# A macaron of attention and sparse layers: the attention body's buffers apart, its norm and q's first part on ScalarE, a PSUM bank cleared sooner, and the first sparse stage's sends in pieces

## Chip, cores and metric

The program runs on one NeuronCore of a Trainium2 chip. The metric is the device time of one execution in microseconds. The core's engines are TensorE (PE), VectorE (DVE), ScalarE (ACT) and GpSimd (POOL), and SyncE (SP), which here only issues DMAs. Each engine runs its own list of instructions in order and waits on semaphores.

## The reference, cut to what matters

Eight sequences of 512 tokens, 128 features, float32. Six stages run one after the other, each on `x + stage(layernorm(x))`: a sparse layer (eight experts of hidden size 512, top 2 of a softmax router), an attention (16 heads of size 8), the sparse layer again, a second sparse layer (16 small experts and a shared one), a state-space layer, and the second sparse layer again. The change touches the first two.

```python
q = (x @ Wq + bq)                      # 16 heads of 8
k = ((x @ Wk + bk) @ Wl + bl)
v = ((x @ Wv + bv) @ Wl + bl)
attn = softmax(q @ k^T * scale); out = (attn @ v) @ Wo + bo
# sparse layer
probs = softmax(xf @ w_router); topk_w, topk_idx = top_k(probs, 2)
h = gelu(xf @ w1[i] + b1[i]); out = sum over the two experts of weight * (h @ w2[i] + b2[i])
```

## The kernel before, in words

`PHASES` lists the stages; each is a function that gives every engine its part of the program. `after_phases` makes an engine wait for the end of the stage before.

**First sparse stage (`moe0_phase`, `occ == 0`).** Tokens are sorted to experts. For each of the eight sequences b, DVE takes the norm's sums (`seq_stats`, step `st`b), POOL makes from them the scale and shift (`seq_root`, four instructions), ACT writes the normalised rows (`seq_xn`, `xn`b), PE transposes them (`seq_T`), ACT copies that out (`seq_copy`, `c`b), PE multiplies by the router weights (`seq_R`) and ACT copies the logits (`seq_logits`, `l`b). The sequences form three groups: 0 and 1; 2 to 4; 5 to 7. For a group DVE picks the top two (`pick_a`, `pick_b`, step `pk`), PE adds up positions (`group_pos`), ACT copies them (`group_copy`, `p`), and DVE computes each token's row in the sorted buffer (`place_a`, `place_b`, step `sl`, L478 to L506) and updates the tables (`place_c`). POOL then sends the group's rows (`group_send`, L535): one indirect DMA for each tile of 128 tokens and each of its two experts, 16, 24 and 24 of them. The buffer was first filled with zeros by a DMA from SP (L2260), for which `group_send` waits (`pads`). The lists PE_STEPS, ACT_STEPS and DVE_STEPS give the order, from which the waits' numbers are made. When all rows have landed, SP loads blocks of 512 rows (`x_load`), 23 in all, and the experts' matmuls run (`up0`, `down0`). Before that DVE splits the expert weights in two parts (`w_lo_dve`, L620).

**Attention (`attn_phase`).** It has two parts. In the first, here called the front, the loop over b runs `pe_a`, `act_a`, `dve_a`, `pool_a` and `sp_a`: POOL gathers the expert results (`gather`, L260), DVE adds them to x (`combine`, L273) and takes the norm's sums (`norm_a`), POOL the root (`norm_b`, L183 and L185), DVE writes the normalised rows (`norm_c`, L215), PE transposes them (`norm_pe`, L223) and multiplies by the weights (L1358, L1364, L1367), ACT adds biases (L1382), and q and k are each split into three bfloat16 parts (`split_q` on DVE, L1401 to L1405; k with its first two parts on ACT, L1411 and L1415, and the rest in `split_k1` and `split_k2`, L1419 and L1423). SP writes the parts to a scratch in DRAM (`saved`) and reads them back rearranged (`load`); for a body it issues 24 such loads, in the first four bodies. Where DVE has time, it already takes row maxima of sequence 0 (`early`, L1596). The second part, the body (`pe_b`, `act_b`, `dve_b`), alternates score matmuls (L1638, L1590), exponentials on ACT (L1646), row maxima on DVE (L1596) and the product with v (`av_pe`, L1656). The tiles of the body (`probs`, `o_sb` and others) lie over the front's (`q_sb`, `parts` and others): `new_part()` frees the latter. So ACT, DVE and POOL wait between the two until the last parts are saved:

```python
for c_ in "qk":
    nc.scalar.wait_ge(saved[c_], 16 * B)
```

PE waits there for `zeroed`, since DVE clears PSUM bank 6 (L1456) behind its last work in the front.

## Time and profile before

| | us |
|---|---|
| median of three runs | 1734.02 |
| the three runs | 1730.81, 1735.60, 1734.02 |
| the profiled execution, its own time | 1741.21 |
| its span | 1739.5 |

The times of rows count from the start of the span. Stages by the trace: routing and sends of the first sparse stage up to 132 us, its experts up to 290, attention's front from 311 to 441, its body from 441 to 852, then the other stages. In a timeline row the brackets hold how long the engine stood idle before the instruction and what released it. Lines are those of the kernel before; the helper's line L535 is the send in both sparse stages.

### The profile page before, as it was taken

Reading aid. Unit: us, or ns where it says so; the run is one execution under the profiler, and the core shown is the slowest. Engines: PE = TensorE matmul, PEld = TensorE weight load, DVE = VectorE, ACT = ScalarE, POOL = GpSimd, SP = SyncE. Lnnn points to the kernel's source line nnn. Section 1 sums busy time; section 2 is a strip of 40 time slices with the busy share of each in tenths; the row PEclk is TensorE's granted clock in tenths of the full one; section 3 lists DMA queues with packets and bytes.
Section 4 is the critical chain, followed back from the end, with each engine's and each line's share of the span. In section 5 each row is a group of like instructions: output and inputs, shape, how many; then the busy total and the mean of one; then the engine's idle time right before and its main releaser. Section 6 shows DMA issues by size and latency. Waiting matters only on the chain. (4 is left out here: it accounts for less than half of the span.)

```text
span 1739.5 us, 20323 instructions
## 1 busy us (share of the span) xinstructions
PE 1292.5 (74%) x6213; PEld 740.0 (43%) x6213; DVE 1227.1 (71%) x2698; ACT 852.9 (49%) x1293; POOL 479.2 (28%) x597
## 2 busy tenths in 40 slices
PE   3208996556788888887539991788798994579998
PEld 3206885222122222222238881555464432446665
DVE  3526995688799999895459984576766665657765
ACT  3206774222677777777437771323333474223332
POOL 3773333761000012222353334434201101111010
PEclk9999998767799999999669995899998855789999
DMA  6152221341111111101222211444340000033444
GB/s 237 59 154 74 81 79 61 96 133 58 38 38 33 35 41 46 38 25 38 68 91 67 86 61 49 91 93 107 78 99 1 0 1 0 1 72 77 98 95 102
DMA packets 83569, 117.31 MB, mean 67 GB/s; under 512 B 16660, under 2 KB 38644, under 8 KB 83468
## 3 DMA queue, kind: packets, MB, share of 16 engines
q1 hardware_dynamic: 75276, 99.28, 21.4%
q0 software_dynamic: 8192, 16.79, 3.4%
q8 instruction: 49, 0.80, 0.2%
q14 instruction: 52, 0.43, 0.1%
HBM read 80.13 MB, written 35.39 MB: 66 GB/s over the span
## 5 line engine op out<-in xcount | busy, mean ns | idle before, releaser
L1596 DVE TENSOR_REDUCE shared<-pair 128x2 f32<-128x1024 f32 x256 | 305.2, 1218 | 28.9 <-PE pair L1590 23.8
L1646 ACT ACTIVATE shared<-pair 128x1024 f32<-128x1024 f32 x256 | 258.8, 1023 | 83.1 <-PE pair L1638 79.5
L730 DVE TENSOR_TENSOR shared<-shared 128x512 fp32r<-128x512 f32 x184 | 175.7, 956 | 30.6 <-ACT shared L720 27.4
L1138 ACT ACTIVATE shared<-pair 128x512 f32<-128x512 f32 x144 | 85.7, 595 | 210.2 <-PE pair L1090 206.2
L535 POOL DMA_INDIRECT xs_rows<-shared,slots x128 | 132.8, 1037 | 128.5 <-ACT shared L1646 78.5
L1149 DVE TENSOR_TENSOR shared<-shared,pair 128x512 f32<-128x512 f32 x128 | 87.5, 684 | 106.2 <-ACT shared L1138 101.1
L1088 PE MATMUL pair<-shared 128*128 128x512 f32 x288 | 149.7, 520 | 17.0 <-DVE shared L1149 16.8
L684 PE MATMUL pair<-shared 128*128 128x512 f32 x368 | 152.9, 415 | 0.0
L1656 PE MATMUL bank<-shared 128*9 128x512 f32 x1024 | 143.1, 632 | 8.8 <-ACT shared L1646 8.7
L714 ACT ACTIVATE shared<-pair,shared 128x512 f32<-128x512 f32 x184 | 126.8, 691 | 43.8 <-PE pair L686 37.5
L260 POOL DMA_INDIRECT staged<-ys_rows,slots x128 | 130.5, 1019 | 61.8 <-issue 36.7
L686 PE MATMUL pair<-shared 128*128 128x512 f32 x368 | 145.7, 396 | 0.0
L685 PE MATMUL pair<-shared 128*128 128x512 f32 x368 | 145.3, 395 | 0.0
L1166 PE MATMUL pair<-shared,down_w 128*128 128x512 f32 x256 | 135.9, 614 | 7.7 <-DVE shared L1156 7.6
L1590 PE MATMUL pair<-shared 48*128 48x512 bf16 x512 | 103.4, 404 | 43.1 <-DVE shared L1596 22.7
L1638 PE MATMUL pair<-shared 51*128 51x512 bf16 x512 | 103.8, 405 | 39.2 <-DVE shared L1596 30.2
L1090 PE MATMUL pair<-shared 128*128 128x512 f32 x288 | 116.9, 406 | 0.0
L1089 PE MATMUL pair<-shared 128*128 128x512 f32 x288 | 116.5, 404 | 0.0
L1638 PEld LDWEIGHTS pair<-shared 51*128 51x128 bf16 x512 | 25.0, 94 | 183.5 <-issue 88.7
L1156 DVE TENSOR_TENSOR shared<-shared 128x512 f32<-128x512 f32 x128 | 87.6, 685 | 10.4 <-DMA shared<-p_coef_rows 10.4
L223 PE MATMUL bank<-ident,xn 128*128 128x128 f32 x128 | 24.5, 324 | 89.8 <-DVE xn L215 87.5
L636 PE MATMUL bank<-ident,shared 128*128 128x128 f32 x184 | 29.5, 286 | 75.5 <-DMA shared<-xs_rows 69.6
(290 smaller groups left out, 2398.1 us busy)
## 6 DMA issues: line engine op xcount, KB each, us to landing
shared<-p_coef_rows SPq DMA_DIRECT2D x64, 512.0 KB, 10.2
shared<-xs_rows SPq DMA_DIRECT2D x46, 256.0 KB, 2.8
ys_rows<-shared SPq DMA_DIRECT2D x46, 256.0 KB, 2.0
xs_rows<-shared SPq DMA_DIRECT2D x1, 5888.0 KB, 20.9
staged<-in_L_ffn_w SPq DMA_DIRECT2D x16, 256.0 KB
shared<-in_L_ffn_w SPq DMA_DIRECT2D x16, 256.0 KB
p_q_parts<-shared SPq DMA_DIRECT2D x8, 384.0 KB
p_k_parts<-shared SPq DMA_DIRECT2D x8, 384.0 KB
```

Source lines behind the costliest of these rows:

```text
L260: g.indirect_dma_start(out=buf[:, at:at + E], out_offset=None, in_=ys_rows, in_offset=bass.IndirectOffsetOnAxis(ap=slots[:, b * TILES + i, ...
L535: g.indirect_dma_start(out=xs_rows, out_offset=bass.IndirectOffsetOnAxis(ap=slots[:, t, k:k + 1], axis=0), in_=xn_rows[occ][:, t, :], in_o ...
L684: nc.tensor.matmul(out_bank, w_hi, x_hi, start=start, stop=False)
L685: nc.tensor.matmul(out_bank, w_hi, x_lo, start=False, stop=False)
L686: return nc.tensor.matmul(out_bank, w_lo, x_hi, start=False, stop=stop)
L730: nc.vector.tensor_tensor(hl[u % RING][:], hid[u % RING][:], hh[u % RING][:], ALU.subtract).then_inc(s["dve_done"], 1)
L1088: nc.tensor.matmul(out_bank, w_hi, x_hi, start=start, stop=False)
L1166: nc.tensor.matmul(bank[4 + b % 2][:], w, hid[t % 4][:], start=(j == 0), stop=(j == IT - 1)).then_inc(s["down_done"], 1)
L1596: nc.vector.tensor_reduce(mneg[:, i, 2 * c:2 * c + 2], pair_of("max", b, m)[:], AX_X, ALU.max, negate=True).then_inc(s["mx_read"], 1)
L1638: last = nc.tensor.matmul(pair_of("exp", b, 2 * st + p)[:, f, :], ka[par][rows, c, kt * P:(kt + 1) * P], qa[par][rows, c, :], start=True, ...
L1646: nc.scalar.activation(probs[st % 2][:, 2 * p:2 * p + 2, :], pair_of("exp", b, 2 * st + p)[:], ACT.Exp, scale=scale).then_inc(s["exp_done" ...
L1656: last = nc.tensor.matmul(bank[6][32 * hh:32 * hh + HD + 1, :], v_all[:, b * TILES + kt, hh % 2 * (H // 2) + g * HG // 2 + hh // 2, :], pr ...
```

## The change

In the first sparse stage DVE takes the sums of all eight sequences first, POOL all eight roots before any send, ACT and PE handle the sequences 0 and 1, then 2 and 3, in pairs, and the sends wait at some places for steps of ACT (`pace`) and, before the third group, for `onehot`. SP waits for the first block's landing before it issues the load of the second, in both expert stages of this kind. In attention the body's tiles no longer lie over the front's, and the waits between the parts go; q's first part (the cast at L1401) moves to ACT (`q1_act`), `norm_c` gives way to `xn_a` on ACT behind `k1_act`, for which POOL makes the shift as well (`shift_a`, two instructions more); the clearing of bank 6 moves ahead of DVE's second group of early maxima; and `load` waits for `saved` in the body.

```diff
@@ -333,11 +333,11 @@
 
 
         GROUPS = (((0, 2), (2, 5), (5, 8)), ((0, 2), (2, 4), (4, 6), (6, 7), (7, 8)))
-        PE_STEPS = ("T0 T1 R0 T2 R1 T3 R2 pos0 T4 R3 T5 R4 T6 R5 pos1 T7 R6 R7 pos2 bias".split(),
+        PE_STEPS = ("T0 T1 R0 R1 T2 T3 R2 pos0 T4 R3 T5 R4 T6 R5 pos1 T7 R6 R7 pos2 bias".split(),
                     "T0 R0 T1 R1 pos0 T2 R2 T3 R3 pos1 T4 R4 T5 R5 pos2 T6 R6 pos3 T7 R7 pos4 bias".split())
-        ACT_STEPS = ("xn0 xn1 c0 xn2 c1 l0 xn3 c2 l1 xn4 c3 l2 p0 xn5 c4 l3 xn6 c5 l4 c6 l5 p1 xn7 c7 l6 l7 p2 th bias".split(),
+        ACT_STEPS = ("xn0 xn1 c0 c1 l0 l1 xn2 xn3 c2 c3 l2 p0 xn4 c4 l3 xn5 c5 l4 xn6 c6 l5 p1 xn7 c7 l6 l7 p2 th bias".split(),
...
@@ -755,18 +755,22 @@
                 if occ == 0:
                     t.wait_ge(pool_chain, 9)
                     t.wait_ge(x_first, 32)
-                    for b in range(B):
-                        if b > 1:
-                            t.wait_ge(s["act_step"], act_at(occ, f"c{b - 2}"))
+                    seq_T(occ, 0, bank[0])
+                    seq_T(occ, 1, bank[1])
+                    seq_R(occ, 0, bank[2])
+                    seq_R(occ, 1, bank[3])
+                    t.wait_ge(s["act_step"], act_at(occ, "c0"))
+                    seq_T(occ, 2, bank[0])
+                    for b in range(3, B):
+                        t.wait_ge(s["act_step"], act_at(occ, f"c{b - 2}"))
                         seq_T(occ, b, bank[b % 2])
-                        if b:
-                            if b > 2:
-                                t.wait_ge(s["act_step"], act_at(occ, f"l{b - 3}"))
-                            seq_R(occ, b - 1, bank[2 + (b - 1) % 2])
+                        t.wait_ge(s["act_step"], act_at(occ, f"l{b - 3}"))
+                        seq_R(occ, b - 1, bank[2 + (b - 1) % 2])
                         if b == 3:
                             group_pos(occ, 0, bank[4])
                         if b == 6:
                             group_pos(occ, 1, bank[5])
+                    t.wait_ge(s["act_step"], act_at(occ, f"l{B - 3}"))
                     seq_R(occ, B - 1, bank[3])
                     group_pos(occ, 2, bank[4])
@@ -798,18 +802,19 @@
             def scalar(c_):
                 after_phases(c_, n)
                 if occ == 0:
-                    for b in range(B):
-                        if b != B - 1:
-                            seq_xn(occ, b)
-                        if b in (0, B - 1):
-                            continue
-                        seq_copy(occ, b - 1, bank[(b - 1) % 2])
-                        if b > 1:
-                            seq_logits(occ, b - 2, bank[2 + b % 2])
-                        if b == 4:
-                            group_copy(occ, 0, bank[4])
-                    seq_copy(occ, 6, bank[0])
-                    seq_logits(occ, 5, bank[3])
+                    for b in (0, 2):
+                        seq_xn(occ, b)
+                        seq_xn(occ, b + 1)
+                        seq_copy(occ, b, bank[0])
+                        seq_copy(occ, b + 1, bank[1])
+                        seq_logits(occ, b, bank[2])
+                        if b == 0:
+                            seq_logits(occ, 1, bank[3])
+                    group_copy(occ, 0, bank[4])
+                    for b in range(4, 7):
+                        seq_xn(occ, b)
+                        seq_copy(occ, b, bank[b % 2])
+                        seq_logits(occ, b - 1, bank[2 + (b - 1) % 2])
                     group_copy(occ, 1, bank[5])
                     seq_xn(occ, 7)
                     seq_copy(occ, 7, bank[1])
@@ -853,25 +858,16 @@
                     v.wait_ge(x_first, 32)
                     for b in range(4):
                         seq_stats(v, occ, b)
+                    v.wait_ge(x_rest, 16)
+                    for b in range(4, B):
+                        seq_stats(v, occ, b)
                     v.wait_ge(tables_ready, 2)
-                    pick_a(v, occ, 0)
-                    pick_b(v, occ, 0)
-                    v.wait_ge(x_rest, 16)
-                    seq_stats(v, occ, 4)
                     for G in range(3):
-                        if G == 1:
-                            pick_a(v, occ, 1)
-                            pick_b(v, occ, 1)
-                            seq_stats(v, occ, 7)
-                        if G == 2:
-                            pick_a(v, occ, 2)
-                            pick_b(v, occ, 2)
+                        pick_a(v, occ, G)
+                        pick_b(v, occ, G)
                         place_a(v, occ, G)
                         place_b(v, occ, G)
                         place_c(v, occ, G)
-                        if G == 0:
-                            seq_stats(v, occ, 5)
-                            seq_stats(v, occ, 6)
                 else:
                     seq_stats(v, occ, B - 1)
...
+
+                if what is not None:
+                    g.wait_ge(s["act_step"], act_at(occ, what))
+
             def gpsimd(g):
                 after_phases(g, n)
                 if occ == 0:
                     route_consts(g)
-                    for b in range(B - 1):
+                    for b in range(B):
                         seq_root(g, occ, b)
-                    group_send(g, occ, 0)
-                    seq_root(g, occ, B - 1)
-                    group_send(g, occ, 1)
+                    group_send(g, occ, 0, pace=lambda k, n: routed(g, {4: "l3", 8: "l4", 12: "l5"}.get(k)))
+                    group_send(g, occ, 1, pace=lambda k, n: routed(g, {6: "l6", 12: "l7", 18: "p2"}.get(k)))
+                    g.wait_ge(s["dve_step"], dve_at(occ, "onehot"))
                     group_send(g, occ, 2)
                 else:
                     seq_root(g, occ, B - 1)
@@ -967,7 +968,9 @@
                         q_.wait_ge(s["xT_ps"], NBLK * occ + i - 2)
                     q_.dma_start(xb[i % 3], rows(xs_rows, i)).then_inc(s[f"x_ld{i % 3}"], 16)
 
-                for i in range(7):
+                x_load(0)
+                q_.wait_ge(s["x_ld0"], 16 * (per_ld[0] * occ + 1))
+                for i in range(1, 7):
                     x_load(i)
                 for i in range(NBLK):
                     if i + 7 < NBLK:
...
-
             probs = [view(P, HG * T).rearrange("p (h t) -> p h t", h=HG) for _ in range(2)]
             o_sb = view(P, T)
...
+            def xn_a(f, b):
+
+                nc.scalar.wait_ge(shift_ready, b)
+                nc.scalar.wait_ge(xnT_ps, f)
+                for i in range(TILES):
+                    last = nc.scalar.activation(xn[:, i, :], x_of(b)[:, i, :], ACT.Identity, bias=shift[:, i:i + 1], scale=rs_y[:, i:i + 1])
+                last.then_inc(xn_ready, 1)
+
...
+                q1_act(b, par)
                 biased(K_BANK, "k_ps", k_sb, V_BL, "k_sb", "k_split", b)
                 k1_act(b, par)
+                if not last_:
+                    xn_a(f0 + b + 1, b + 1)
                 for g in parts_due(b):
                     mT_act(0, 0, g)
                 if not last_:
...
 
-                v.wait_ge(s["q_sb"], b + 1)
-                need(v, saved["q"], 16 * b)
-                chain = Chain(v, s["q_chain"], 3)
+                v.wait_ge(s["q_sb"], 2 * b + 2)
+                chain = Chain(v, s["q_chain"], 2)
                 chain.begin(b)
                 p_, r = parts["q"][par], rest["q"]
-                chain(nc.vector.tensor_copy(p_[:, 0, :], q_sb[:]))
                 chain(nc.vector.tensor_tensor(r[:], q_sb[:], p_[:, 0, :], ALU.subtract))
                 chain(nc.vector.tensor_copy(p_[:, 1, :], r[:]))
                 chain.end()
                 nc.vector.tensor_tensor(p_[:, 2, :], r[:], p_[:, 1, :], ALU.subtract).then_inc(s["q_split"], 1)
 
+
+            def q1_act(b, par):
+                nc.scalar.wait_ge(s["q_sb"], 2 * b + 1)
+                need(nc.scalar, saved["q"], 16 * b)
+                nc.scalar.copy(parts["q"][par][:, 0, :], q_sb[:]).then_inc(s["q_sb"], 1)
 
             def k1_act(b, par):
...
                 early_dve(v, b, 0)
-                if not last_:
-                    norm_c(v, f0 + b + 1, b + 1)
                 v.wait_ge(s["v_ps"], b + 1)
                 nc.vector.tensor_tensor(
                     v_all[:, bass.ds(b * TILES, TILES), :, 0:HD], bank[V_BANK][:].rearrange("p (i h d) -> p i h d", i=TILES, d=HD),
                     bl_bc[:].rearrange("p (h d) -> p h d", d=HD).unsqueeze(1).to_broadcast([P, TILES, H, HD]),
                     ALU.add).then_inc(s["v_sb"], 1)
+                if last_:
+                    v.wait_ge(s["v_sb"], B)
+                    nc.vector.memset(bank[6][:], 0.0).then_inc(s["zeroed"], 1)
                 early_dve(v, b, 1)
                 need(v, s["q_split"], b)
                 split_q(v, b, par)
@@ -1452,17 +1469,23 @@
                 early_dve(v, b, 2)
                 if last_:
                     split_k2(v, b, par)
-                    v.wait_ge(s["v_sb"], B)
-                    nc.vector.memset(bank[6][:], 0.0).then_inc(s["zeroed"], 1)
                 if first_:
                     nc.vector.memset(v_all[:, :, :, HD:], 1.0).then_inc(s["zeroed"], 1)
                     nc.vector.memset(ones3, 1.0).then_inc(s["zeroed"], 1)
+
+            def shift_a(f):
+
+                nc.gpsimd.wait_ge(mv_ready, f + 1)
+                nc.gpsimd.tensor_scalar(shift[:], mv[:, :, 0], -1.0, None, ALU.mult)
+                norm_b(f)
+                nc.gpsimd.wait_ge(rs_ready, f + 1)
+                nc.gpsimd.tensor_tensor(shift[:], shift[:], rs_y[:], ALU.mult).then_inc(shift_ready, 1)
 
             def pool_a(b, par, first_, last_):
                 if mixed(n) and b + 2 < B:
                     gather(nc.gpsimd, occ0, b + 2, FIRST_HALF)
                 if not last_:
-                    norm_b(f0 + b + 1)
+                    shift_a(f0 + b + 1)
                 if mixed(n) and b + 2 < B:
                     gather(nc.gpsimd, occ0, b + 2, SECOND_HALF)
 
@@ -1798,6 +1821,8 @@
 
                     nc.sync.wait_ge(s["st_ready"], PER * b + GP * (g + 1))
                     if b + 2 < B:
+                        for c in "qk":
+                            nc.sync.wait_ge(saved[c], 16 * (b + 3))
                         load(b + 2, par, g)
                     if g < GB - 1:
                         m_sp(b + 1, 1 - par, g)
...
                     act_a(b, b % 2, b == 0, b == B - 1)
-                nc.scalar.wait_ge(s["q_split"], B)
-                nc.scalar.wait_ge(s["k_split"], B)
-                nc.scalar.wait_ge(s["v_ps"], B)
-                for c_ in "qk":
-                    nc.scalar.wait_ge(saved[c_], 16 * B)
                 for b in range(B):
                     act_b(b, b % 2, b == 0, b == B - 1)
                 o_act(B - 1, GB - 1)
...
```

POOL's program in the first sparse stage, from the last root ahead of the sends; before:

```order
L390 TENSOR_TENSOR sh_all<-sh_all,rs_all 128x4
L535 DMA xs_rows<-shared,slots 11776x128 x16
L385 TENSOR_SCALAR sh_all<-mv_all 128x4
L386 TENSOR_SCALAR var_all<-mv_all 128x4
L388 TENSOR_TENSOR rs_all<-var_all,neg_half 128x4
L390 TENSOR_TENSOR sh_all<-sh_all,rs_all 128x4
L535 DMA xs_rows<-shared,slots 11776x128 x48
```

and of the change:

```order
L385 TENSOR_SCALAR sh_all<-mv_all 128x4
L386 TENSOR_SCALAR var_all<-mv_all 128x4
L388 TENSOR_TENSOR rs_all<-var_all,neg_half 128x4
L390 TENSOR_TENSOR sh_all<-sh_all,rs_all 128x4
L535 DMA xs_rows<-shared,slots 11776x128 x64
```

The eighth root stands ahead of the first send, and the 64 sends in one row.

ACT's program at the start of the first sparse stage (L395 is `seq_xn`, L409 `seq_copy`, L419 `seq_logits`, L435 `group_copy`); before:

```order
L395 ACTIVATE shared<-x_res,sh_all,rs_all 128x128 x8
L409 COPY xnT<-pair 128x512
L395 ACTIVATE shared<-x_res,sh_all,rs_all 128x128 x4
L409 COPY xnT<-pair 128x512
L419 COPY z_all<-pair 128x32
L395 ACTIVATE shared<-x_res,sh_all,rs_all 128x128 x4
L409 COPY xnT<-pair 128x512
L419 COPY z_all<-pair 128x32
L395 ACTIVATE shared<-x_res,sh_all,rs_all 128x128 x4
L409 COPY xnT<-pair 128x512
L419 COPY z_all<-pair 128x32
L435 COPY pos_g<-pair 128x72
```

and of the change:

```order
L395 ACTIVATE shared<-x_res,sh_all,rs_all 128x128 x8
L409 COPY xnT<-pair 128x512 x2
L419 COPY z_all<-pair 128x32 x2
L395 ACTIVATE shared<-x_res,sh_all,rs_all 128x128 x8
L409 COPY xnT<-pair 128x512 x2
L419 COPY z_all<-pair 128x32
L435 COPY pos_g<-pair 128x72
```

The positions of group 0 (L435) are now copied behind four sequences' rows, where five stood ahead of them.

ACT's program in attention's front, one body; before:

```order
L1382 ACTIVATE shared<-pair,vecs 128x512
L1382 ACTIVATE shared<-bank,vecs 128x512
L1382 ACTIVATE shared<-pair,vecs 128x512 x2
L1411 CAST shared<-shared 128x512
L229 COPY xnT<-bank 128x512
L1415 CAST shared<-shared 128x512
```

and of the change (L1422 is the cast in `q1_act`, L1427 that in `k1_act`, L1385 `xn_a`):

```order
L1392 ACTIVATE shared<-pair,vecs 128x512
L1392 ACTIVATE shared<-bank,vecs 128x512
L1392 ACTIVATE shared<-pair,vecs 128x512
L1422 CAST shared<-shared 128x512
L1392 ACTIVATE shared<-pair,vecs 128x512
L1427 CAST shared<-shared 128x512
L1385 ACTIVATE xn<-x_res,shift,rs_y 128x128 x4
L229 COPY xnT<-bank 128x512
L1431 CAST shared<-shared 128x512
```

The cast of q stands ahead of k's bias, and the four rows of the next sequence's norm between k's first cast and the copy of the transpose.

## Rows read from the trace of the kernel before

**Rows 1.** page, part 1: busy us (share of span) xinstructions

```profile
PE 1292.5 (74%) x6213; PEld 740.0 (43%) x6213; DVE 1227.1 (71%) x2698; ACT 852.9 (49%) x1293; POOL 479.2 (28%) x597
```

**Rows 2.** timeline of PE, 130 to 138 us

```profile
134.90 1.09 PE L636 MATMUL bank<-ident,shared 128*128 128x128 f32 x4 [49.66 <-DMA shared<-xs_rows]
...
137.55 0.66 PE L636 MATMUL bank<-ident,shared 128*128 128x128 f32 x2 [1.56 <-DVE shared L681]
```

**Rows 3.** timeline of POOL, 37 to 131 us: start us, us, engine line op

```profile
37.44 0.24 POOL L385 TENSOR_SCALAR sh_all<-mv_all 128x4 f32<-128x4 f32 x1 [10.12 <-DVE mv_all L378]
...
41.19 0.20 POOL L390 TENSOR_TENSOR sh_all<-sh_all,rs_all 128x4 f32<-128x4 f32 x1
...
42.01 1.23 POOL L535 DMA_INDIRECT xs_rows<-shared,slots  x1 [0.62 <-issue]
...
64.78 1.11 POOL L535 DMA_INDIRECT xs_rows<-shared,slots  x1 [0.49 <-issue]
...
129.73 0.96 POOL L535 DMA_INDIRECT xs_rows<-shared,slots  x1 [0.30 <-issue]
```

**Rows 4.** timeline of DVE, first 40 us

```profile
12.45 0.38 DVE L378 BATCH_NORM_AGGREGATE mv_all<-st_all 128x2 f32<-128x6 f32 x4
...
29.73 0.07 DVE L478 MEMSET next_e<- 128x8 f32 x1 [4.50 <-ACT pos_g L435]
...
33.72 0.18 DVE L506 CAST slots<-slot_f 128x16 uint32<-128x16 f32 x1
```

**Rows 5.** timeline of ACT, first 40 us

```profile
13.29 1.65 ACT L395 ACTIVATE shared<-x_res,sh_all,rs_all 128x128 f32<-128x128 f32 x4 [0.38 <-POOL sh_all L390]
...
14.84 0.56 ACT L409 COPY xnT<-pair 128x512 f32<-128x512 f32 x1
...
29.45 0.21 ACT L435 COPY pos_g<-pair 128x72 f32<-128x72 f32 x1
```

**Rows 6.** DVE groups, 343 to 441 us

```profile
L273 DVE SCALAR_TENSOR_TENSOR x_res<-staged,w_tok,x_res 128x128 f32<-128x128 f32 x40 | 11.4, 346 | 4.3 <-DMA staged<-ys_rows,slots 4.1
...
L215 DVE TENSOR_SCALAR xn<-x_res,mv,rs_y 128x128 f32<-128x128 f32 x20 | 5.8, 361 | 1.6 <-POOL rs_y L185 1.6
...
L1401 DVE CAST shared<-shared 128x512 bf16<-128x512 f32 x6 | 2.6, 441 | 0.1
```

**Rows 7.** ACT groups, 311 to 441 us: | busy, mean ns | idle before

```profile
L1411 ACT CAST shared<-shared 128x512 bf16<-128x512 f32 x8 | 4.9, 618 | 18.0 <-DMA p_k_parts<-shared 17.9
```

**Rows 8.** timeline of PE, 434 to 442 us

```profile
440.66 0.61 PE L1638 MATMUL pair<-shared 51*128 51x512 bf16 x2 [7.17 <-DVE bank L1456]
```

**Rows 9.** timeline of ACT, 438 to 445 us

```profile
442.30 1.28 ACT L1646 ACT_TABLE_LOAD   x1 [5.76 <-DMA p_k_parts<-shared]
```

**Rows 10.** timeline of DVE, 438 to 445 us

```profile
438.92 0.68 DVE L1423 TENSOR_TENSOR shared<-shared 128x512 bf16<-128x512 f32 x1
...
442.22 1.23 DVE L1596 TENSOR_REDUCE shared<-pair 128x2 f32<-128x1024 f32 x1 [2.02 <-DMA p_k_parts<-shared]
```

**Rows 11.** timeline of PE, first 40 us

```profile
14.99 1.12 PE L402 MATMUL pair<-ident,shared 128*128 128x128 f32 x4 [0.84 <-ACT shared L395]
...
15.90 1.72 PE L414 MATMUL pair<-wr,xnT 128*128 128x8 f32 x8
```

**Rows 12.** timeline of SP's queue, first 60 us

```profile
4.93 2.39 SPq L2260 DMA_DIRECT2D xs_rows<-shared  x1
```

**Rows 13.** DMA issues, 0 to 60 us: KB each, us to landing

```profile
xs_rows<-shared SPq DMA_DIRECT2D x1, 5888.0 KB, 20.9
...
x_res<-in_L_attn_x SPq DMA_DIRECT2D x2, 0.5 KB, 6.7
```

**Rows 14.** page, part 6: DMA issues, xcount, KB each, us to landing

```profile
shared<-xs_rows SPq DMA_DIRECT2D x46, 256.0 KB, 2.8
```

**Rows 15.** windows: each engine busy (xcount), then PEclk, DMA share, GB/s

```profile
446.00:450.00 4.00, 3.99 (x18) 0.41 (x14) 2.17 (x3) 2.23 (x3) 0.00 (x0) 0.50 0.01 3
...
454.00:460.00 6.00, 4.93 (x38) 1.11 (x36) 5.62 (x9) 4.47 (x6) 0.00 (x0) 1.00 0.13 32
```

21 lines of the change are left out of this document (7 added, 14 removed).

## The prediction

> **What bounds the kernel now.** I read the page's busy times first: no engine fills the span, PE is busy 74% of it and DVE 71% [rows 1]. So each stage has its own limit, and the change can only pay where a wait ends last. Then I read the timelines of the two stages that it touches.
>
> In the first sparse stage the experts' first transpose starts at 134.90, after PE stood idle for 49.66 us, released by the load of the sorted rows [rows 2]. That load follows the last send, which ends at 129.73 + 0.96 = 130.69 [rows 3]. From the first send at 42.01 on, POOL issues one send after the other, save for one root that stands between the groups. So POOL's sends are the path, and what counts is when the first one starts. Its rows (`slots`) were ready at 33.72 + 0.18 = 33.90 [rows 4]; POOL was still at the roots of sequences 5 and 6, 37.44 to 41.39, and had waited 10.12 us for DVE's sums [rows 3], which stood in DVE's order behind the placing of group 0. That is 8 us lost. DVE's placing in turn waited 4.50 us for the copy of the positions [rows 4], which ACT made at 29.45 [rows 5], behind a fifth sequence.
>
> In attention the front goes through three limits: gathers in the first bodies (DVE waited 4.1 us for them after 343) [rows 6], the saves of k to DRAM in ACT's order (17.9 us of ACT's waits) [rows 7], then DVE with its early maxima. At the end of the front DVE finishes the last split at 438.92 + 0.68 = 439.60, PE's first score matmul comes at 440.66 after the clearing of the bank, and ACT and DVE go on only at 442.30 and 442.22, both released by the landing of the last saved k [rows 8 to 10].
>
> **The sends.** Followed through the new order with the old durations. Sequence 1's rows are written by 13.29 + 1.65 = 14.94 [rows 5]; its transposes end at 16.1, router products of 0 and 1 (1.72 for one) follow each other from 15.90 and end near 19.2 [rows 11], so its logits are there at 19.4. ACT then writes sequences 2 and 3 (3.2), PE transposes the latter (1.1), ACT copies (0.6), PE multiplies sequence 2 meanwhile and ACT copies its logits: 25.4. The picks and the position sums are done long before, so the positions' copy ends near 25.8 where it was 29.66. Placing takes 33.90 - 29.73 = 4.17 [rows 4], and the first send starts 0.2 after: 30.2.
>
> Three other things must be ready by then. The second half of x was issued ahead of the zero fill at 4.93 [rows 12] and took about 6.7 [rows 13]: there before 12, when DVE ends its fourth sums at 12.83 [rows 4]. The zero fill lands at 4.93 + 20.9 = 25.8 [rows 12, 13]. The eight roots: that of sequence 1 released ACT at 13.29 [rows 5], one root takes about 2.0 (two in 37.44 to 41.39) [rows 3], so the other six end by 25.4. None holds the send. First send 42.01 - 30.2 = 11.8 earlier; and the root between the groups, 2.0 and its gap of 0.2, leaves the path, since all stand ahead. The 64 sends with the rest of their gaps take what they took, 88.7 - 2.2 = 86.5, so the last ends at 116.7 instead of 130.69: **-14.0**.
>
> The new waits between the sends cost nothing: each further sequence needs about 1.65 + 1.1 + 0.6 + 1.7 = 5 on ACT and PE, so `l3` comes near 30.5, `l7` before 50, and `p2` and the tables before 60, while the fifth send is due at 30.2 + 4 x 1.35 = 35.6, the thirty-fifth at 76 and the third group at 84. What hides them is a queue of sends; if it ran dry, the sends would wait for ACT, 5 us for each sequence. The weights and their splits move up by about 25 us with DVE's order and stay ahead of the loads. The bounds of this term: if the positions' copy gained nothing, the first send would start at 34.2, -7.8 - 2.2 = -10.0; if only the roots and the fill held it, at 25.8, -18.4. I keep to the chain of the rows.
>
> **The first block's load.** SP issues the second load only when the first has landed, near 134.9, and it needs about 2.8 [rows 14]: 137.7. PE takes it at 137.55 today, and then waited for DVE, not for the load [rows 2]. So +0.2; against it the first load no longer shares the DMA engines with two others. I take 0, bounds -0.5 and +0.5 in each of the two stages.
>
> **Attention's front.** Per body, POOL gets two instructions more, as those of 0.24 and 0.20 at 37.44 and 41.19 [rows 3], with gaps 0.6, and they lie in a loop: gathers land, DVE combines and takes sums, POOL makes the root, then issues the next gathers. ACT writes the rows in 1.65 [rows 5] where DVE took 4 x 0.361 = 1.44 [rows 6]. In the three bodies held by the gathers this is on the path: about +2 in all. Behind `xn_a` on ACT are the copy of the transpose and k's second cast; ahead of it is `k1_act` with its wait for the saved k, so PE's next sequence starts up to 2 later in the bodies held by the saves. DVE loses 1.44 and the cast of 0.44 [rows 6] per body, 1.9, which pays where DVE is the limit, the last four bodies. But there DVE then waits for PE's v product, so I book a third, 0.65 for each, -2.6. The front's end moves by -0.6. Bounds: all 1.9 in four bodies, -5.6 with the +2; none, +2.
>
> **Between front and body.** With buffers of its own the body need not wait for the saves. ACT ended its last cast at 442.30 - 5.76 = 436.54 [rows 9]; 0.6 earlier, plus the table load of 1.28, gives a first exponential at 437.2 against 443.58: -6.3. DVE can start at 439.1 against 442.22 [rows 10]: -3.1. PE is no longer held by the clearing, which lay 7.17 us of idle back [rows 8]: it now lies ahead of maxima that PE issues anyway. The scores go round three bank pairs, for which both an exponential and a maximum must be done; the later one is DVE's, but DVE is busy only 2.17 of 4 us in the stretch behind [rows 15] and catches up. Between the ends I take **-5.2** for front and border together, nearer ACT's; the bounds are -2 and -8. Everything behind it is a chain of stages and moves as a whole. The shift's new count in the later stage and the wait in `load` change no order: the saves they ask for have landed by then.
>
> **Sum.** -14.0 + 0 - 5.2 = -19.2. The profiled execution took 1741.21 with a span of 1739.5, so it would be 1722.0; it stands 7.2 above the median of the runs, 1734.02, to which I refer the forecast: **1714.8**. About 0.3%, 5.2 us, is what a measurement of this kernel can tell from no change.
>
> **Rivals.**
> - *The positions come no sooner.* If PE's or ACT's new order holds the copy at 29.66, the sends give -10.0, and the time is 1734.0 - 10.0 - 5.2 = 1718.8. For it: seven waits in a row between two engines; against it: each is in the rows. 0.10.
> - *The front eats the border.* The +2 of the gathers, and DVE's relief lost behind PE, and each body's norm behind `k1_act`: front and border together 0, 1720.0. For it: ACT's waits for saves, 17.9 us [rows 7], now delay PE as well. 0.17.
> - *The clock does not fall.* At the body's start PE runs at a granted clock of 0.50, its level of 1.2 GHz, and does 18 matmuls in 4 us, 4.5 per us; later at 1.00 it does 38 in 6, 6.3 per us [rows 15]. It had been idle 7.17 us before [rows 8]. The new gap is some 3 to 4. If the clock stays up, the 8 us between the starts of these two windows shrink to 5.7: -2.3 more, 1712.5. 0.17. The Trainium skill, "TensorE: Matmul & The Clock Gate", Part 1, says that an idle TensorE is given the lower clock and a busy one the higher; by it the shorter gap may keep the clock, and the sum would be -21.5 rather than -19.2; no row here shows a gap of 3 us at that place.
> - *Slower.* ACT becomes the front's pacemaker: each of seven bodies pays all of it, 1.65 for the rows, 0.6 for q's cast, 0.6 on POOL, 2.8, or 19.6, and the last `k1_act` waits so late that the border gives nothing: -14.0 + 19.6 = +5.6, 1739.6. It decides from 2.0 a body on. Against it: DVE, not ACT, is the limit in the last four bodies, where it sheds 1.9 us for each. 0.03.
>
> The forecast has 0.48, and 0.05 is left for what I don't see. Its own range is 1711 to 1718; with the rivals, and the runs' own scatter of 2 or 3 us, 1706 to 1723. Faster by over 0.3%: 0.94; within it: 0.03; slower: 0.03.
>
> **What would show it.** First send near 30 and no gap over 0.5 us between sends; last send ended near 117; the first expert transpose near 121. Attention's front as long as before within 3 us; the table load at once behind ACT's last cast; the body's first exponential some 6 us earlier relative to the front's start, the steady rhythm unchanged. Wrong would make it: a first send after 34, sends stretched by the weights' traffic, or bodies of the front longer by 2 us.

## The result, and the profile after

The changed kernel took 1723.68 us, median of 20 runs (1716.65 to 1734.12); the kernel before took 1734.01 beside it, median of 20 (1726.04 to 1744.04). The ratio is 0.9938, its 95% interval 0.9921 to 0.9956, so between 7.6 and 13.7 us less. The forecast was 1714.8 with a range up to 1723, so the median lies 0.7 us above its upper end: the direction was right, the gain was about half of the 19.2 us that the sum gave. The profiled execution took 1726.33 with a span of 1724.6, against 1739.5 before.

The page of the changed kernel, part 1 (busy us, share of the span, instructions), which answers to [rows 1]:

```profile
PE 1303.0 (76%) x6213; PEld 745.0 (43%) x6213; DVE 1216.7 (71%) x2662; ACT 868.8 (50%) x1329; POOL 484.2 (28%) x611
```

PE and DVE are as busy as before, in a shorter span: what went is waiting. Now the first sparse stage. First POOL's sends (start us, duration, line, and in brackets the idle time and what ended it), then ACT and PE in the same stretch, all from the timeline of the changed kernel:

```profile
30.69 1.23 POOL L535 DMA_INDIRECT xs_rows<-shared,slots  x1 [4.86 <-DVE slots L506]
...
65.12 0.96 POOL L535 DMA_INDIRECT xs_rows<-shared,slots  x1 [0.30 <-issue]
69.87 0.96 POOL L535 DMA_INDIRECT xs_rows<-shared,slots  x1 [3.79 <-ACT z_all L419]
...
81.34 5.55 POOL L535 DMA_INDIRECT xs_rows<-shared,slots  x1 [0.30 <-issue]
...
119.87 0.95 POOL L535 DMA_INDIRECT xs_rows<-shared,slots  x1 [0.30 <-issue]
```

```profile
43.72 0.59 ACT L409 COPY xnT<-pair 128x512 f32<-128x512 f32 x1 [1.27 <-PE pair L402]
54.72 0.19 ACT L419 COPY z_all<-pair 128x32 f32<-128x32 f32 x1 [10.41 <-issue]
69.41 0.19 ACT L419 COPY z_all<-pair 128x32 f32<-128x32 f32 x1 [14.51 <-remote]
```

```profile
43.48 3.42 PE L414 MATMUL pair<-wr,xnT 128*128 128x8 f32 x16
...
124.92 1.09 PE L636 MATMUL bank<-ident,shared 128*128 128x128 f32 x4 [40.74 <-DMA shared<-xs_rows]
127.69 1.12 PE L636 MATMUL bank<-ident,shared 128*128 128x128 f32 x4 [1.68 <-DMA shared<-xs_rows]
```

The first send starts at 30.69 where it was 42.01 [rows 3]: forecast 30.2. From there one send follows the other, with gaps of 0.30, until 66.08. Then POOL stands still for 3.79 us, released by ACT's copy of sequence 7's logits (L419), `l7`: the wait that the forecast had booked at nothing. PE did the router products of sequences 6 and 7 from 43.48 to 46.90, and they should have been copied at once, as those of sequence 5 were (products until 39.43, copy at 39.47); the copies come at 54.72 and 69.41. The last send ends at 119.87 + 0.95 = 120.82, against 130.69 before and 116.7 in the forecast. Of these 4.1 us, 0.5 is the later start and 3.5 the stop (3.79 less the usual 0.30). The long send at 81.34 is not new: before there was one of 5.25. The first expert transpose stands at 124.92 where it was 134.90 [rows 2], the second, held by the second load, 2.77 behind it where it was 2.65.

The first transpose of attention's front stands at 301.18 where it was 311.29, 10.1 earlier. In the front the second sequence, and the border to the body:

```profile
311.10 0.25 POOL L1479 TENSOR_SCALAR shift<-mv 128x4 f32<-128x4 f32 x1 [0.50 <-issue]
311.41 0.23 POOL L183 TENSOR_SCALAR var<-mv 128x4 f32<-128x4 f32 x1
311.73 1.37 POOL L185 TENSOR_TENSOR rs_y<-var,neg_half 128x4 f32<-128x4 f32 x1
313.17 0.25 POOL L1482 TENSOR_TENSOR shift<-shift,rs_y 128x4 f32<-128x4 f32 x1
313.46 1.65 ACT L1385 ACTIVATE xn<-x_res,shift,rs_y 128x128 f32<-128x128 f32 x4 [2.60 <-POOL shift L1482]
315.16 1.11 PE L223 MATMUL bank<-ident,xn 128*128 128x128 f32 x4 [5.47 <-ACT xn L1385]
...
426.33 0.62 ACT L1431 CAST shared<-shared 128x512 bf16<-128x512 f32 x1 [5.16 <-DVE shared L1435]
426.97 1.28 ACT L1669 ACT_TABLE_LOAD   x1
```

The second transpose comes 13.98 behind the first; before it was 12.80 (324.09 - 311.29). POOL's root with the shift takes 311.10 to 313.42, ACT writes the rows in 1.65, PE transposes. From the first to the last of the eight transposes it takes 107.1 us where it took 103.9. At the border the table load stands right behind ACT's last cast, without the 5.76 us of [rows 9], and the first exponential follows 20 us after the last transpose where it was 28.4. Front and border together gave 5.2 us in this pair of traces, to the tenth what was booked; such a match is luck, since traces of one kernel differ by more (below).

The clock, in windows (us, busy time and count by engine, granted clock of PE, DMA share, GB/s):

```profile
412.00:418.00 6.00, 5.25 (x16) 1.97 (x16) 4.26 (x8) 1.46 (x3) 0.00 (x0) 0.68 0.30 101
418.00:424.00 6.00, 3.54 (x22) 1.69 (x18) 5.73 (x7) 3.11 (x6) 0.00 (x0) 0.89 0.09 30
424.00:430.00 6.00, 2.88 (x12) 0.66 (x13) 5.79 (x12) 3.64 (x4) 0.00 (x0) 0.50 0.19 66
430.00:434.00 4.00, 3.27 (x18) 0.46 (x16) 3.50 (x4) 1.89 (x3) 0.00 (x0) 0.50 0.31 103
434.00:438.00 4.00, 3.73 (x20) 0.50 (x16) 2.45 (x2) 1.94 (x2) 0.00 (x0) 0.50 0.01 2
438.00:441.00 3.00, 2.73 (x20) 0.50 (x16) 1.84 (x2) 1.94 (x2) 0.00 (x0) 0.70 0.00 0
441.00:444.00 3.00, 2.34 (x20) 0.48 (x16) 2.62 (x7) 1.94 (x2) 0.00 (x0) 1.00 0.05 17
```

PE falls from 0.89 to 0.50, its level of 1.2 GHz, and comes back to 1.00 by 441, some 13 us after the first exponential at 428.26; before, it was back by 454, some 10 after 443.58 [rows 15]. The 0.89 of 418 to 424 puts the fall near 422.7, before the body's first score matmul at 424.39; PE's wait of 2.58 us, its longest from 418 to 430, comes later and ends at 427.58. And the clock had been down before: the mean granted from 412 to 418 was 0.68. So it fell inside the front, with no wait over 1.94 us from 418 up to the fall, and the gap at the border was not what decided it.

### The profile page after: what moved, and what is told of

It is laid out like the page before. It is cut to its first block and busy times, and to the rows that moved or that the text cites. A ratio compares the mean times of both kernels' runs of the same rounds, so it can differ in the third digit from the quotient of the medians.

```text
span 1724.6 us, 20362 instructions
## 1 busy us (share of the span) xinstructions
PE 1303.0 (76%) x6213; PEld 745.0 (43%) x6213; DVE 1216.7 (71%) x2662; ACT 868.8 (50%) x1329; POOL 484.2 (28%) x611
## 3 DMA queue, kind: packets, MB, share of 16 engines
q1 hardware_dynamic: 75276, 99.28, 21.7%
## 5 line engine op out<-in xcount | busy, mean ns | idle before, releaser
L1619 DVE TENSOR_REDUCE shared<-pair 128x2 f32<-128x1024 f32 x256 | 305.1, 1218 | 25.0 <-PE pair L1613 20.9
L730 DVE TENSOR_TENSOR shared<-shared 128x512 fp32r<-128x512 f32 x184 | 175.8, 956 | 30.9 <-ACT shared L720 27.7
L1152 DVE TENSOR_TENSOR shared<-shared,pair 128x512 f32<-128x512 f32 x128 | 87.5, 684 | 106.3 <-ACT shared L1141 103.4
L223 PE MATMUL bank<-ident,xn 128*128 128x128 f32 x128 | 24.6, 325 | 98.7 <-DVE xn L215 74.1
L1159 DVE TENSOR_TENSOR shared<-shared 128x512 f32<-128x512 f32 x128 | 87.7, 685 | 10.4 <-DMA shared<-p_coef_rows 10.4
L908 POOL CAST shared<-shared 128x1024 fp32r x46 | 49.0, 1065 | 120.5 <-PE pair L686 120.5
## 6 DMA issues: line engine op xcount, KB each, us to landing
shared<-p_coef_rows SPq DMA_DIRECT2D x64, 512.0 KB, 10.3
xs_rows<-shared SPq DMA_DIRECT2D x1, 5888.0 KB, 21.1
```

Source lines behind the costliest of these rows:

```text
L730: nc.vector.tensor_tensor(hl[u % RING][:], hid[u % RING][:], hh[u % RING][:], ALU.subtract).then_inc(s["dve_done"], 1)
L1619: nc.vector.tensor_reduce(mneg[:, i, 2 * c:2 * c + 2], pair_of("max", b, m)[:], AX_X, ALU.max, negate=True).then_inc(s["mx_read"], 1)
```

## The experiments

Sixteen runs, four at a time on one chip; differences are against the kernel before on the same chip. Each chip had one such set of four, so a chip and a point in time can't be told apart here. "l6" and "l7" are ACT's copies of the logits of sequences 6 and 7 (L419), "stop" is POOL's longest idle time between sends, "T0" the first expert transpose, "front" attention's first to last transpose, "border" from there to the first exponential, all in the one trace of each kernel.

| kernel | chip | us against before (by the ratio, interval) | l6, l7 | stop | T0 | front + border |
|---|---|---|---|---|---|---|
| before | - | 0 | 68.8, 70.5 | 2.5 | 134.90 | 103.9 + 28.4 |
| changed | - | -10.8 (-13.7 to -7.6) | 54.7, 69.4 | 3.8 | 124.92 | 107.1 + 20.0 |
| e1_sends_only | A | -11.8 (-15.9 to -7.5) | 44.1, 45.8 | none | 120.41 | 105.3 + 28.3 |
| e2_attention_only | A | -4.0 (-8.0 to -0.2) | 68.8, 70.5 | 2.5 | 135.53 | 107.1 + 19.8 |
| e3_no_pace | A | -19.4 (-24.8 to -13.9) | 44.1, 45.8 | none | 120.27 | 106.3 + 20.6 |
| e4_l7_early | A | -18.2 (-22.7 to -13.9) | 44.3, 46.1 | none | 122.03 | 104.4 + 20.5 |
| c1_changed_again | B | -9.9 (-14.9 to -4.9) | 61.2, 62.7 | 3.3 | 123.44 | 105.8 + 20.9 |
| c2_changed_third | B | one run | 61.3, 62.8 | 3.2 | 123.54 | 106.1 + 21.4 |
| e5_norm_on_vector | B | -6.1 (-10.3 to -2.1) | 58.8, 79.8 | 13.3 | 133.34 | 104.4 + 23.2 |
| e6_gathers_3_1 | B | -4.9 (-8.3 to -1.2) | 60.3, 82.0 | 13.5 | 133.41 | 111.3 + 21.6 |
| c3_no_pace_again | C | -6.6 (-10.2 to -3.1) | 57.3, 78.3 | 12.5 | 132.95 | 106.7 + 20.1 |
| c4_l7_early_again | C | -16.7 (-21.7 to -11.5) | 56.4, 56.5 | 3.5 | 126.09 | 103.0 + 21.1 |
| e7_shifted_stream | C | one run | 74.1, 86.7 | 18.3 | 138.50 | 106.2 + 20.7 |
| e8_sends_held | C | one run | 44.5, 46.2 | held | 136.96 | 105.0 + 19.9 |
| c5_changed_beside | D | -15.3 (-18.9 to -11.5) | 55.9, 69.9 | 4.5 | 126.47 | 106.0 + 21.6 |
| c6_l7_early_beside | D | -15.5 (-20.3 to -10.4) | 53.2, 56.0 | 3.3 | 124.02 | 105.9 + 21.4 |
| e9_root_between | D | -16.0 (-21.0 to -11.1) | 57.4, 59.1 | 2.5 | 124.03 | 106.7 + 21.6 |
| c7_before_traced | D | one run | 69.1, 70.8 | 2.5 | 134.92 | 102.3 + 27.7 |

**The two parts apart, the waits taken away, one wait earlier.** e1 is the kernel before with the diff down to the line of the first load's wait, e2 with the rest of it. The edits of the other two:

```
# e3_no_pace, on the changed kernel
-group_send(g, occ, 0, pace=lambda k, n: routed(g, {4: "l3", 8: "l4", 12: "l5"}.get(k)))
-group_send(g, occ, 1, pace=lambda k, n: routed(g, {6: "l6", 12: "l7", 18: "p2"}.get(k)))
+group_send(g, occ, 0)
+group_send(g, occ, 1)
# e4_l7_early, on the changed kernel
-... {6: "l6", 12: "l7", 18: "p2"} ...
+... {2: "l7", 18: "p2"} ...
```

> The kernel before with the first sparse stage's edits alone (orders of PE, ACT and DVE, the roots ahead of the sends, the waits between the sends, the wait behind the first load). If the sends gave what the trace of the changed kernel shows, the first expert transpose comes at about 124.9 instead of 134.90, the rest of the program keeps its length, and the time is 10 us below the kernel before. The gap between the sends for the logits of sequence 7 (3.79 us in the trace of the changed kernel) should stand there again if it belongs to this stage's order; if it was an accident of one execution, the sends end 3.5 us sooner, near 117.3, and the time is 13.5 below.

> The kernel before with the attention edits alone. Theory: the two parts add. The front's last transposes come about 3 us later after the front's start than before (103.9 us, now near 107.1) and the first exponential stands 20 us behind them where it stood 28.4, so the time is 5 to 6 us below the kernel before. Rival: the attention gain needs the earlier sends' timing (what the DMA queues carry then) and alone gives 0.

> The changed kernel without the waits between the sends (l3, l4, l5, l6, l7, p2); the wait before the third group stays. Theory A, ACT's late copies of the logits of sequences 6 and 7 (54.72 and 69.41, 8 and 22 us after PE ended their products) have nothing to do with the sends: only the wait for l7 goes, the last send ends 3.5 us sooner, near 117.3, and the time is 3.5 below the changed kernel. Theory B, a running stream of sends holds ACT off until the stream pauses: without a pause the logits of sequence 7 come only when the second group's 40 sends end, about 81.3 plus 3.3 = 84.6; the picks, the positions (4.9) and the placing (about 5.5) follow, so the third group begins near 95 instead of 88.5, POOL stands still for some 13 us, and the time is 4 to 8 us above the changed kernel.

> The changed kernel with the wait for l7 ahead of the third send of the second group, near 53.5, instead of ahead of its thirteenth; l6 and l7 of PE are done by 46.9. Theory A (ACT is late for a reason of its own): the sends stand still from 53.5 until 69.4, 15 us, of which 3.5 stood there before, and the time is 12 above the changed kernel. Theory B (the pause lets ACT through): the logits of sequence 7 come 3 to 4 us after the sends stop, near 57, the third pick, the tables and the weights' splits move up by 12 us, and the sends end where they ended, near 120.8 (within 1 us).

ACT in e1_sends_only, in whose first stage nothing differs from the changed kernel:

```profile
44.12 0.19 ACT L419 COPY z_all<-pair 128x32 f32<-128x32 f32 x1 [0.92 <-PE pair L414]
45.83 0.19 ACT L419 COPY z_all<-pair 128x32 f32<-128x32 f32 x1 [1.52 <-PE pair L414]
```

Here the logits come at 44.12 and 45.83, 0.92 us and 1.52 us after ACT was free, and no send waits. The last send ends at 116.32 and the first expert transpose stands at 120.41: -14.5, the forecast's term (116.7, -14.0). The chain of steps from the old rows was sound; what it lacked does not happen on this chip. So e3 and e4 could not tell theory A from B here. The two parts add within the intervals: -11.8 and -4.0, and e3, which has both and no stop, -19.4 (-24.8 to -13.9).

**The changed kernel again, and two kernels on attention.** e5 and e6 build on e3.

```
# e5_norm_on_vector
 dve_a:  early_dve(v, b, 0)
+        if not last_: norm_c(v, f0 + b + 1, b + 1)
 act_a:  k1_act(b, par)
-        if not last_: xn_a(f0 + b + 1, b + 1)
 pool_a: -shift_a(f0 + b + 1)   +norm_b(f0 + b + 1)
 moe1:   -shift0 = (B - 1) * (occ + 1)   +shift0 = (B - 1) * occ
# e6_gathers_3_1
 pool_a: -gather(..., b + 2, FIRST_HALF)    +gather(..., b + 2, (0, 3))
          shift_a(f0 + b + 1)
         -gather(..., b + 2, SECOND_HALF)   +gather(..., b + 2, (3, TILES))
```

> The changed kernel, unedited, once more. Theory A, the lateness of the logits of sequences 6 and 7 in its trace was an accident of that execution: the copies come near 44 and 46, the sends run without the 3.8 us gap, the last send ends near 116.4, and the time is 14 to 19 us below the kernel before. Theory B, it belongs to this kernel: the copies come at 50 to 70 again, the sends end near 120.8, and the time is again 10 below.

> The changed kernel a third time, one look. As for the second: copies of the logits near 44 and 46 and a last send near 116.4 if the lateness is an accident of single executions; at 50 to 70 and near 120.8 if it belongs to this kernel.

> The changed kernel without the waits between the sends (e3_no_pace) and with the rows of the norm written by DVE again, so that POOL computes no shift and ACT writes no rows in attention's front. Theory, in the bodies held by the gathers the norm's new path costs about 1.3 us each (POOL's two more instructions, a power of 1.36 instead of 1.05, ACT's 1.65 against 1.3), and DVE's relief pays only in the last bodies: the first five transposes stand about 12.8 us apart instead of 14.1, the fifth comes 5 us earlier after the front's start, the last ones lose 3 to 5 again, and the time is within 2 us of e3_no_pace. Rival, the relief of DVE carries the gain of the border: the front ends as in the kernel before, and the time is 3 us or more above e3_no_pace.

> e3_no_pace with six of a body's eight gathers ahead of POOL's part of the norm instead of four. Theory, these bodies are a loop: norm on POOL 2.3, four gathers 5.3, landing 2.7, DVE's combine and sums 3.6; with two gathers behind the norm the loop is 11.4 and POOL's own work (8 gathers and the norm, 12.6) is the limit, so the first five transposes stand about 12.7 us apart instead of 14.1, and the front is 4 to 5 us shorter there; the last bodies, held by DVE, may give 1 or 2 of it back. Time 2 to 5 us below e3_no_pace. Rival, the last bodies' limit is fixed by other work (saves, DVE), and nothing remains: same time as e3_no_pace.

On this chip ACT is late in all four. In both runs of the changed kernel POOL stops at the wait for l6, at 58.4, and the copy comes 2.8 us into the stop; l7 follows 1.5 behind. Without the waits (e5, e6) l7 comes only about when the second group of sends is through (at 79.79 with the last send ended at 80.93 in e5, at 82.00 with 80.86 in e6), and the third group then has to wait for the picks, the placing and the tables:

```profile
79.97 0.96 POOL L535 DMA_INDIRECT xs_rows<-shared,slots  x1 [0.30 <-issue]
94.21 5.10 POOL L535 DMA_INDIRECT xs_rows<-shared,slots  x1 [13.27 <-DVE shared L628]
```

That is theory B of e3: the waits between the sends cost 3 to 4 us where ACT is late, and without them it would be 13.

For attention, e5 shows what the norm on ScalarE is worth: nothing that can be seen. Front and border take 127.6 us, and the thirteen traces with the change's attention as it stands take 124.0 to 128.3. Of its two parts the border, 23.2, is longer than in any of them (19.8 to 21.6); the front, 104.4, lies among theirs (103.0 to 107.1), so the shorter front that the expectation named is not shown. What gained is what e5 keeps: the buffers apart, the bank cleared sooner, and q's first cast on ACT; these three were not tried one by one.

e6 failed, and usefully. Its second transpose comes 16.1 us after the first, since six gathers now stand ahead of the norm; after that the rhythm is 13.3 and 12.5, as expected, and then 19.1. There POOL has no idle time between its gathers and its norm; the norm alone keeps the gathers apart, from 347.80 to 349.99. And the timeline shows the same lateness as in the sends. PE first, then ACT:

```profile
351.56 0.66 PE L223 MATMUL bank<-ident,xn 128*128 128x128 f32 x4 [3.46 <-ACT xn L1385]
```

```profile
355.28 0.58 ACT L229 COPY xnT<-bank 128x512 f32<-128x512 f32 x1 [3.77 <-remote]
```

PE's transpose ends at 352.22, ACT's copy of it starts at 355.28, 3.1 later, after 3.77 of idle time. In c3 (below) the gathers lie 3.61 us apart at this place, 345.94 to 349.55, and the copy is on time (351.83).

**What is late: the sends taken away, ACT's instructions shifted.** c3 and c4 are e3 and e4 unedited.

```
# e7_shifted_stream, on e3: on ACT, behind the first group's positions
+for i_ in range(24):
+    nc.scalar.copy(th_all[:, i_ // NE0, i_ % NE0:i_ % NE0 + 1], sh_all[:, 0:1])
# e8_sends_held, on e3: on POOL, ahead of the first send
+g.wait_ge(s["act_step"], act_at(occ, "l7"))
```

> e3_no_pace once more, unedited. On one chip its logits of sequence 7 came at 45.78 and it was 19 us below the kernel before; two kernels with the same first stage had them at 79.79 and 82.00 on another chip, the third group waited 13.3 and 13.5 us, and the sends ended at 129.5. Theory, the lateness goes with the chip: this run shows the one or the other, and the same in every kernel of this call. Rival, it goes with the single execution: the kernels of this call differ among themselves.

> e4_l7_early once more, unedited. Where ACT is late (logits of sequence 7 later than 50 without a pause): if a pause of the sends lets ACT through, POOL stops at about 53.5, the logits come 3 us later, near 56 and 57.5, POOL goes on by 58, and the sends end near 119.5, as with the waits of the changed kernel (119.3 and 119.5 on the chip where it was late); if ACT is late for a reason of its own, the sends stand for 20 us. Where ACT is on time: sends end at 116.3 to 118, as before.

> e3_no_pace with 24 one-column copies (into a tile that is written later anyway) ahead of the rows of sequence 4 on ACT. Theory, what is late is the supply of ACT's instructions: an instruction transfer of 8 KB followed ACT's last logits copy within 1 us in each trace, wherever that came (46, 63, 70, 80, 83); with 24 instructions more ahead it comes that much earlier in the order, behind sequence 5 or 6, and where ACT is late, the lateness starts at an earlier copy than that of sequence 6. Rival, it is the semaphores from PE: the same copies, of sequences 6 and 7, are late, and the instruction transfer stays behind the last logits copy.

> e3_no_pace with the first send held until the logits of sequence 7. If the stream of sends is what holds ACT off, these logits come near 44 to 47 on any chip, and the sends start there, 15 to 16 us later than in e3_no_pace, and end near 132. If ACT is late for another reason, they come at 55 or later where the other kernels of this call have them late, and the sends start later still.

This chip is of the late kind too. ACT with the sends held, and ACT with 24 instructions more ahead while the sends run:

```profile
44.49 0.19 ACT L419 COPY z_all<-pair 128x32 f32<-128x32 f32 x1 [0.92 <-PE pair L414]
46.20 0.19 ACT L419 COPY z_all<-pair 128x32 f32<-128x32 f32 x1 [1.52 <-PE pair L414]
```

```profile
45.35 0.24 ACT L435 COPY pos_g<-pair 128x104 f32<-128x104 f32 x1 [3.35 <-remote]
53.80 0.58 ACT L409 COPY xnT<-pair 128x512 f32<-128x512 f32 x1 [6.66 <-remote]
74.10 0.18 ACT L419 COPY z_all<-pair 128x32 f32<-128x32 f32 x1 [19.72 <-remote]
86.70 0.18 ACT L419 COPY z_all<-pair 128x32 f32<-128x32 f32 x1 [12.42 <-remote]
```

Without sends ACT is on time (44.49, 46.20), on the very chip on which it idles 12.8 and 20.8 us before these copies with them (c3). It takes the stream of sends.

e7 speaks against the supply of ACT's instructions. In e3's trace an instruction transfer of 0.01 MB lies in the 3 us behind l7; with 24 instructions more it lies at 28 to 31, long ahead. The views of the DMA queues, of e3 for 45 to 48 and of e7 for 28 to 31 (queue, kind: packets, MB, share):

```profile
q14 instruction: 1, 0.01, 0.7%
```

```profile
q14 instruction: 1, 0.01, 0.9%
```

From 30 until 94 no other transfer of that queue shows in e7. So ACT had its instructions early, and was later than ever: 6.66, 19.72 and 12.42 us of idle time. One sign that the expectation gave to the supply theory did come: the lateness starts at an earlier copy than sequence 6's. But c4, without the 24 instructions, has that copy late too (46.48, after 3.93 of idle time), and in e7 it stands some 2 us later in the stream. Each late one waits for PE: T7 to its copy, R6 and R7 to theirs. Notices between other engines came at once: in c3 l7 ends at 78.52 and DVE's pick starts at 78.60; DVE's sums end at 82.76 and PE's positions start at 82.82; from PE's positions, ended at 83.17, to ACT's copy at 86.03 it is again 2.9, although the last send had ended at 80.98.

The trace also records when a semaphore's count rose, and that settles on which side the time goes. In e5 the count that ACT's copies wait for rises at 58.77 for R6 and at 79.76 for R7, whose products' record ends at 47.19; the copies start at 58.79 and 79.79. So ACT starts 0.02 to 0.03 us after it is told, and what is late is PE's update of the semaphore, for R7 by 32.6 us behind the record's end. In the same stretch nearly every recorded update by ACT and DVE comes 0.01 us behind its instruction's end. On chip A no update by PE is over 0.2 us late before the program's end; in each of the other traces some are, outside this stage too and in the kernel before as well: in c7 by 1.62 at 360.0 and by 1.41 at 1180.3, both behind a row of gathers by POOL.

Two rivals stay open. A transfer of 0.02 MB on another instruction queue, q8, lies near T7 in the traces of the changed kernel, e3, c3 and c4 (42 to 46), e7 (48) and e9 (54), so on chip A too; no run moved it apart from PE's work. And the recording may take part: the four traces of chip A hold 5626 to 5638 updates by engines, all others 5370 to 5419, so there some records are missing. It is not the traced execution alone, for the medians of c3 and c4 differ by 9.2 us where T0 in their traces differs by 6.9; but no run shows an execution without the profiler.

c4 shows the pause at work: POOL stops at 53.48, l6 and l7 come 2.9 us later, POOL goes on at 56.94. The sends end at 121.96, not near 119.5 as expected, because they take longer themselves: 68.9 us in sum against 66.5 in c1. On this chip the one early wait is worth 9 us against none (1720.61 and 1729.78), and the two intervals against the kernel before lie apart.

**What remained open: the root, the place of the wait, the trace of before.** e9 is e3 with sequence 7's root where the kernel before had it:

```
 for b in range(B - 1): seq_root(g, occ, b)
 group_send(g, occ, 0)
+seq_root(g, occ, B - 1)
 group_send(g, occ, 1)
```

> The changed kernel, unedited, on the same chip as the three below. Where ACT is late, the traces so far have the first expert transpose at 123.4 to 124.9 with attention's front and border 6 us shorter, so 16 to 17 us below the kernel before; the timed runs gave 10. Theory, the cost of the waits between the sends varies from execution to execution (two of the three traces stopped at l6, one at l7): the trace is near 124 and the median again about 10 below, with a wide spread. Rival, the trace of the kernel before is a slow one: then its second trace (c7) has shorter stages, and the median is 15 below or more on a fresh chip.

> e4_l7_early beside the changed kernel on one chip. One wait, for l7 ahead of the second group's third send, in place of l6 and l7 at its seventh and thirteenth. Theory, one early pause lets both copies through and none is left for later: sends end at 118 to 122, time 16 to 18 us below the kernel before on a chip of either kind, 4 to 7 below the changed kernel. Rival, the two are the same within 2 us, and the differences between calls were the chips'.

> e3_no_pace with sequence 7's root between the two first groups of sends, where the kernel before had it; no waits between the sends. Theory, the stretch without sends that this root makes (2.2 to 2.5 us, 50.9 to 53.1) is what kept ACT on time in the kernel before: the lateness from PE to ACT ends there, the logits of sequences 6 and 7 come near 57 and 59, the third group is ready in time, and the sends end near 119, the first expert transpose near 122.5, on any chip. Rival, a pause without a wait is too short: where ACT is late, the logits of sequence 7 come only when the second group ends, near 80, the third group waits over 8 us, and the sends end near 129.

> The kernel before, unedited, for a second trace of it. The first expert transpose comes near 134.9 and attention's front and border take 132 to 134 us again; logits of sequences 6 and 7 near 68.8 and 70.5, if the root's pause keeps ACT on time there too. The stages that no edit touches (attention's body 415.7, the dense stage behind it 457.5) show how far the first trace was from a usual one: 5 us less in both together would put the rest of the difference between the traces and the medians there.

The late kind again (c5: l7 at 69.91, a stop of 4.5). ACT in e9_root_between:

```profile
57.44 0.19 ACT L419 COPY z_all<-pair 128x32 f32<-128x32 f32 x1 [0.92 <-issue]
59.14 0.19 ACT L419 COPY z_all<-pair 128x32 f32<-128x32 f32 x1 [1.52 <-PE pair L414]
```

Both copies are on time, 0.92 and 1.52 us after ACT was free, as on the chip of e1. POOL issues no send from 50.96 to 53.47. Ahead of that stretch PE's update for group 1's positions comes 0.8 late, as in the other late traces; behind it all are on time, the last, for group 2's positions, at 64.00, eight sends on. The kernel before has the same stretch, and its copies are on time here as well (69.12, 70.83 in c7). So the root between the groups, which the forecast took off the path for a gain of 2.2, kept the rest of the stage going. But it does two things: it leaves a stretch without sends, and it moves the work of sequence 7 behind it, for R6 and R7 run from 55.69 to 59.11, where in the traces without it they end before 50 (e7: 56.4). Which of the two was needed is not shown, and e9 has no copy that was already waiting when the stretch began. In e6 a stretch of 2.19 us, the norm, did not prevent a late copy.

c7's trace of the kernel before has the first expert transpose at 134.92, but front and border 129.9 instead of 132.3, and a span of 1733.0 instead of 1739.5. The first trace was a slow one by some 6 us, as the rival of c5 has it. c6 was expected 4 to 7 us below the changed kernel and is 1.8 below, its rival's "the same within 2 us". Changed, early wait and root between lie within their intervals of each other: no version here is shown to beat the changed kernel beside it; c6 and e9 are as fast with fewer waits.

## Why the prediction was wrong, by its own steps

**The sends: the first send was right, the step that failed is "The new waits between the sends cost nothing".** The first send was forecast at 30.2; it came at 30.3 to 30.7 in every trace of the new order but e8's, where it was held. The length of 64 sends was right too: on chip A the last one ends at 116.3 in e1 and e3. But the sentence that each further sequence needs 5 us on ACT and PE, and that `l7` therefore comes before 50, took the notice from PE for immediate. While POOL sends without a pause it is not, on three chips of four: PE's updates came up to 23 us behind the products in the changed kernel's four traces, `l7` at 62 to 70, the sends stopped for 3.2 to 4.5 us, and the stage gave 8.4 to 11.5 us instead of 14.0. The rest of that spread is the sends' own length, 66.5 to 68.7 us in sum. "What hides them is a queue of sends" had it upside down: with the sends held back (e8) nothing was late, so the queue of sends is what made them late. Also wrong, and without a price here: tables and splits near 60. In the changed kernel's trace PE's first product for the tables comes at 81.58, before at 82.64: 1 us earlier, not 25; on chip A it came at 58.30.

**The root between the groups.** Booked at -2.2 as pure loss. Where PE's notices are late the changed kernel stops about as long elsewhere, so this term was about zero there; only on chip A was it earned.

**The first block's load** was booked at 0, with +0.2 at its second block: the second transpose came 0.12 later behind the first.

**Attention's front.** Booked -0.6: +2 for the gathers, -2.6 of DVE's relief. The loop of gathers, combine and norm lost 1.2, 1.7, 0.7 and 1.1 us in the four bodies it holds, 4.7, more than twice the price: POOL's part grew from 1.37 (308.54 to 309.91 in the trace before) to 2.32, that is 0.95 a body and not 0.6, since its power (L185) took 1.37 instead of 1.05; what the rest of it was no run shows. The last three gave back 1.5. So +3.2 in place of -0.6 in this pair of traces, and +2.0 in the means of all: 105.9 in the thirteen with the change's attention, 103.8 in the three with the old one (before, c7, e1).

**The border.** Booked -4.6 of the -5.2; it gave -8.4: the 5.76 of waiting went, as said, and DVE's relief in the last body, which I had booked in the front, shows here, since it brings ACT's last cast forward (its start 18.0 behind the last transpose, before 20.7); e5, with the norm back on DVE, loses about 2 of it. Front and border together are -5.2 against the first trace of before and -2.9 against the second; the means of the same thirteen and three traces are 126.6 and 132.0, -5.4; e2 alone was timed at -4.0 (-8.0 to -0.2). The mechanism and the sum were right, the split between the two was not.

**Rivals.** "The clock does not fall": it fell, but inside the front, before the border's gap, so that gap did not decide it, and these runs do not test what the forecast took from the Trainium skill, "TensorE: Matmul & The Clock Gate", Part 1. "The front eats the border": half true, the front lost 3.2 and the border paid it. "The positions come no sooner": no. The rival that happened, sends held by the new waits, was named among what would make the forecast wrong only as "sends stretched", with no chance of its own. The Trainium skill, "Perfetto Trace Analysis", "Tensor Engine Instruction (MATMUL, LD_WEIGHTS)", says that PSUM's acknowledgement sends the semaphore update, after the matmul's reported end, and that this end is an estimate. The traces agree in that PE's records look done while the semaphore's count rises up to 32.6 us later (e5); the page names no such delay, and whether it lies before or behind the acknowledgement no run here shows.

**The total.** The four traces of the changed kernel have T0 at 124.6 on average, -10.3, and front and border at 127.2 against 131.1 in the two traces of before, -3.9. That makes -14.2, and their spans differ by 13.9. The medians differ by 10.3, 9.3 and 16.9 on the three chips. So of the missing 8.9 us, 3.7 lie in the sends. Attention has 1.3 by these six traces and none by all sixteen. The remaining 4 to 5 us I can't settle: parts that hardly an edit touches differ between traces by more (attention's body 413 to 421.5, what follows it 865 to 878), and whether the untraced executions stopped longer than the traced ones was not seen.
